# Attention over eight query blocks: own slots for the score pieces, rotating PSUM buffers, unrolled rows

## What is computed

```python
cq = jnp.einsum('bcd,bqd,d->bcq', c, q, w_cq) + b_cq
s = (c @ w_c + b_c)[:, :, None] + (q @ w_q + b_q)[:, None, :] + cq
a = jax.nn.softmax(s, axis=2)
c2q_att = jnp.einsum('bcq,bqd->bcd', a, q)
b_att = jax.nn.softmax(jnp.max(s, axis=2), axis=1)
q2c_att = jnp.einsum('bc,bcd->bd', b_att, c)[:, None, :]
x = jnp.concatenate([c, c2q_att, c * c2q_att, c * q2c_att], axis=-1)
z = x @ W_l.T + b_l
```

## Time and profile before

| | us |
|---|---|
| median of three runs | 265.16 |
| lowest, highest | 263.92, 265.46 |
| the profiled execution | 264.06 |
| its span, first to last instruction | 262.2 |
| mean granted TensorE clock | 0.895 of full |

### The profile page before, as it was taken

How to read it: one execution, slowest core, us unless ns; L and a number is a source line. 1 busy time by engine, 2 the same in 40 slices (tenths; PEclk the granted TensorE clock), 3 DMA queues, 4 the chain that set the end, 5 groups by cost and what they waited for, 6 DMA issues and landing times.

```text
span 262.2 us, 5174 instructions
## 1 busy us (share of the span) xinstructions
PE 198.8 (76%) x1721; PEld 145.0 (55%) x1721; DVE 175.6 (67%) x363; ACT 153.0 (58%) x233; POOL 136.8 (52%) x185
## 2 busy tenths in 40 slices
PE   0349699379969999999999998699841007999990
PEld 0113266236746766667666666599741006988880
DVE  2997887348979979799799796977745001545340
ACT  2289398167849788698686995892020002845430
POOL 2359999892960923907509259960001720244433
PEclk9997997869999999999999999799955555999997
DMA  6995199099998999999999989799000237000000
GB/s 230 401 347 155 40 242 266 22 226 199 248 214 207 246 221 257 242 249 253 240 256 254 257 201 257 107 228 192 0 0 0 100 125 238 4 32 17 17 23 0
DMA packets 127135, 44.68 MB, mean 170 GB/s; under 512 B 107734, under 2 KB 124910, under 8 KB 127118
## 3 DMA queue, kind: packets, MB, share of 16 engines
q1 hardware_dynamic: 126104, 42.87, 69.3%
q0 software_dynamic: 864, 1.58, 1.8%
q10 hardware_dynamic: 150, 0.00, 0.0%
HBM read 14.15 MB, written 4.01 MB: 69 GB/s over the span
## 4 chain that ended last, share of the span: by engine, by line
PE 41%; POOL 16%; issue 13%; DVE 12%; ACT 8%; DMA 7%; ACTq 0%; DVEq 0%; POOLq 0%
POOL qn L408 8%; ACT Pf L566 6%; PE psS L1116 5%; PE psO L927 5%; PE psX L927 4%; DVE S L701 3%; PE psS L912 3%; DMA PT<-Phl 3%; PE psS L914 3%; PE psS L913 3%; POOL rows_by_expert L505 3%; PE psO L930 2%; PE psS L1098 2%; PE psX L930 2%; PE psS L1101 2%
## 5 line engine op out<-in xcount | busy, mean ns | idle before, releaser
L701 DVE TENSOR_SCALAR_CACHE_REDUCE S<-psS 128x1024 f32<-128x1024 f32 (+1 forms) x56 | 61.8, 1105 | 22.5 <-ACT Pf L566 15.5
L566 ACT ACTIVATE Pf<-S,negb 128x1024 f32<-128x1024 f32 (+1 forms) x56 | 59.1, 1056 | 26.5 <-DVE negb L710 21.1
L719 DVE TENSOR_TENSOR Phl<-Pf,Phl 128x1024 f16<-128x1024 f32 x41 | 55.6, 1356 | 2.4 <-ACT Phl L582 2.4
L912 PE MATMUL psS<-qTh,gh 128*128 128x512 f16 (+1 forms) x104 | 40.3, 388 | 19.5 <-issue 6.3
L582 ACT CAST Phl<-Pf 128x1024 f16<-128x1024 f32 x48 | 50.2, 1045 | 7.7 <-DMA PT<-Phl 5.9
L445 POOL TENSOR_TENSOR Phl<-Pf,Phl 128x256 f16<-128x256 f32 x28 | 17.9, 671 | 48.0 <-ACT Phl L582 47.7
L913 PE MATMUL psS<-qTl,gh 128*128 128x512 f16 (+1 forms) x104 | 40.4, 388 | 0.0
L914 PE MATMUL psS<-qTh,gl 128*128 128x512 f16 (+1 forms) x104 | 40.4, 388 | 0.0
L927 PE MATMUL psO<-qn,PT 128*128 128x256 f16 x204 | 39.1, 284 | 0.0
L930 PE MATMUL psO<-qn,PT 128*128 128x128 f16 x204 | 37.3, 226 | 0.0
L927 PE MATMUL psX<-qn,PT 128*128 128x256 f16 x204 | 36.2, 273 | 0.0
(11 more groups left out here) (179 smaller groups left out, 373.6 us busy)
## 6 DMA issues: line engine op xcount, KB each, us to landing
stageT<-in_w SPq DMA_DIRECT2D x8, 512.0 KB, 4.3
stageT<-in_ctxT SPq DMA_DIRECT2D x6, 512.0 KB, 6.7
PT<-in_ctx SPq DMA_DIRECT2D x6, 512.0 KB, 6.8
rows_by_expert<-stageT SPq DMA_DIRECT2D x5, 385.5 KB, 3.5
S<-rows_by_expert SPq DMA_DIRECT2D x3, 514.0 KB, 6.0
PT<-Phl SPq DMA_TRANSPOSE x48, 4.0
Pf<-in_x SPq DMA_DIRECT2D x1, 512.0 KB, 4.0
stageT<-in_x SPq DMA_DIRECT2D x1, 512.0 KB, 4.4
```

The costliest lines, as they stand in the source:

```text
L566: nc.scalar.activation(Pf[:, e % 3, 0:b - a], S[:, a:b], ACT.Exp, bias=negb[:, bass.ds(t, 1)], accum_out=Lp[:, bass.ds(t * NG + e, 1)]).th ...
L701: nc.vector.tensor_scalar(out=S[:, a:b], in0=psS[n % 3][:, 0:b - a], scalar1=1.0 / GS, scalar2=None, op0=ALU.mult, op1=ALU.max, accum_out= ...
L719: nc.vector.tensor_tensor(lo, Pf[:, e % 3, 0:hi.shape[1]], hi, ALU.subtract).then_inc(low_done, 1)
L912: nc.tensor.matmul(dst, g_h, qTh[:, a:b], start=True, stop=False)
```

## The change

- `S` becomes a ring of SLOTS = 8 long slots, with two short ones (`Send`) for the short pieces. exp works in place; `Pf` is gone. An eviction waits for the low half eight long pieces back.
- `Phl` has PARTS = 4 buffers instead of three.
- PSUM buffers rotate over the whole sequence of pieces (`(u * NG + n) % 3`), so each score piece waits for the eviction three pieces back, across rows too.
- Weighted sums follow twelve pieces behind (AHEAD = 5 in the place of LAG = 4).
- DVE does `low(u-1, n-1)` ahead of `scores(u, n)`; the row's maximum comes right behind the last eviction, the short low half behind that. `attended` moves to the start of a row.
- POOL takes the low half of piece 3 only for rows 1 to 6 (0 to 6 before); in row 0 it is DVE's.
- The loops are written out on all engines.
- The fill of expert rows is issued ahead of the short transpose, not behind it. Some later buffers (`hf`, `x2T`, `xTp`, `wc2`, `ints`, `x_sb`) lie elsewhere.

```diff
@@
-    LAG = 4
+    AHEAD = 5
+    SLOTS = 8
+    PARTS = 4
+    BANKS = 3
@@
-        S = sb("S", [P, Q])
-        Pf = sb("Pf", [P, 3, GR])
-        Phl = sb("Phl", [P, 3, 2, GR], F16)
+        S = sb("S", [P, SLOTS, GR])
+        Send = sb("Send", [P, 2, QE])
+        Phl = sb("Phl", [P, PARTS, 2, GR], F16)
@@
+        def pool_low(t, e):
+            return e == 3 and 0 < t < T - 1
+        def slot(t, e):
+            return S[:, (t * (NG - 1) + e) % SLOTS, :] if e < NG - 1 else Send[:, t % 2, :]
+        def bank(u, n):
+            return psS[(u * NG + n) % BANKS]
@@ sync
-                if 1 <= t <= NB // RING:
-                    sp.wait_ge(empty_ready, 2)
...
+                    elif e == 5 and 1 <= t <= NB // RING:
+                        sp.wait_ge(empty_ready, 2)
...
@@ gpsimd
-            for e in LOW_POOL:
-                low_piece(0, e)
@@ scalar, exp_piece
-                if e >= 3:
-                    wait_low(act, t, e - 3)
-                elif not isinstance(t, int) or t > 0:
-                    wait_low(act, t - 1, (NG - 1, 4, 5)[e])
-                nc.scalar.activation(Pf[:, e % 3, 0:b - a], S[:, a:b], ACT.Exp, bias=negb[:, bass.ds(t, 1)],
+                nc.scalar.activation(slot(t, e), slot(t, e), ACT.Exp, bias=negb[:, t:t + 1],
@@ scalar, high
-                elif e >= 3:
-                    act.wait_ge(pT_landed[e - 3], 16 * (t + 1))
-                elif has_prev:
-                    act.wait_ge(pT_landed[e + 3], 16 * t)
+                elif past >= 0:
+                    act.wait_ge(pT_landed[past % (NG - 1)], 16 * (past // (NG - 1) + 1))
@@ vector, scores
-                if has_prev:
-                    dve.wait_ge(exp_done, (u - 1) * NG + n + 1)
-                    if n == 0:
-                        dve.wait_ge(negb_ready, u)
+                past = u * (NG - 1) + n - SLOTS
+                if n == NG - 1 and u >= 2:
+                    wait_low(dve, u - 2, n)
+                elif n < NG - 1 and past >= 0:
+                    wait_low(dve, past // (NG - 1), past % (NG - 1))
+                if u > 0 and n == 0:
+                    dve.wait_ge(negb_ready, u)
@@ vector, the rows
-                for e in range(NG):
-                    if e == LAG and has_prev:
-                        attended(t - 1, 1 - odd)
-                    if has_next:
-                        scores(t + 1, e, True)
-                    low(t, e)
-                if has_next:
-                    row_max(t + 1)
...
+            for u in range(1, T):
+                for n in range(NG):
+                    if n > 0:
+                        low(u - 1, n - 1)
+                    elif u > 1:
+                        low(u - 2, NG - 1)
+                    scores(u, n)
+                    if n == 0 and u > 2:
+                        attended(u - 3)
+                row_max(u)
+                if u == 1:
+                    dve.wait_ge(row_term_in_psum, 1)
+                    nc.vector.tensor_copy(row_term[:, :], psX[:, 0:T]).then_inc(row_term_ready, 1)
+            low(T - 2, NG - 1)
...
+            attended(T - 3)
@@ tensor, scores
-                    if n >= 3:
-                        pe.wait_ge(scores_out, u * NG + n - 2)
-                    elif has_prev and n == 0:
-                        pe.wait_ge(scores_out, u * NG)
-                dst = psS[n % 3][:, (c % 2) * CH:(c % 2) * CH + b - a]
+                if c % 2 == 0 and u * NG + n >= BANKS:
+                    pe.wait_ge(scores_out, u * NG + n - BANKS + 1)
+                dst = bank(u, n)[:, (c % 2) * CH:(c % 2) * CH + b - a]
@@ tensor, the rows
-            with pe.Fori(1, T - 2, 2) as t:
-                step(t, 1, True, True)
-                step(t + 1, 0, True, True)
+            for u in range(1, T):
+                if u == 2:
+                    pe.wait_ge(row_term_ready, 1)
+                    pe.wait_ge(late_gl_ready, 1)
+                for n in range(NG):
+                    if u == 1 and n == 3:
+                        row_terms()
+                    for c in range(2 * n, min(2 * n + 2, NCH)):
+                        scores(u, c)
+                    if n >= AHEAD:
+                        weighted(u - 1, n - AHEAD)
+                    elif u > 1:
+                        weighted(u - 2, NG - AHEAD + n)
@@ tensor, behind the rows
-            weighted(T - 2, 0, 3, True)
+            weighted(T - 2, 2)
+            weighted(T - 2, 3)
```

More of the change, by code:

```diff
@@ L370, in _ @@
                 for e in range(NG):
-                    transpose(t, e, t > 0)
+                    transpose(t, e)
                     if e == 2 and t < 2:
@@ L441, in low_piece @@
                 pool.wait_ge(high_done, t * NG + e + 1)
-                _, hi, lo, _ = piece(e)
+                _, hi, lo, _ = piece(t, e)
                 for a in range(0, GR, CHUNK):
                     r = slice(a, a + CHUNK)
-                    last = nc.gpsimd.tensor_tensor(lo[:, r], Pf[:, e % 3, r], hi[:, r], ALU.subtract)
+                    last = nc.gpsimd.tensor_tensor(lo[:, r], slot(t, e)[:, r], hi[:, r], ALU.subtract)
                 last.then_inc(low_pool_done, 1)
-            for e in LOW_POOL:
-                low_piece(0, e)
             pool.wait_ge(b12_landed, 64)
@@ L576, in high @@
                     act.wait_ge(consts_ready, 4)
-                elif e >= 3:
-                    act.wait_ge(pT_landed[e - 3], 16 * (t + 1))
-                elif has_prev:
-                    act.wait_ge(pT_landed[e + 3], 16 * t)
-                _, hi, _, _ = piece(e)
-                nc.scalar.copy(hi, Pf[:, e % 3, 0:hi.shape[1]]).then_inc(high_done, 1)
-            def step(t, has_prev):
+                elif past >= 0:
+                    act.wait_ge(pT_landed[past % (NG - 1)], 16 * (past // (NG - 1) + 1))
+                _, hi, _, _ = piece(t, e)
+                nc.scalar.copy(hi, slot(t, e)).then_inc(high_done, 1)
+            for t in range(T):
                 for e in range(NG):
                     exp_piece(t, e)
-                    high(t, e, has_prev)
-            step(0, False)
-            with act.Fori(1, T - 1) as t:
-                step(t, True)
-            for e in range(NG):
-                exp_piece(T - 1, e)
-                high(T - 1, e, True)
-                if e == 2:
-                    act.wait_ge(nM_ready, 1)
-                    nc.scalar.activation(eb[:, :], Mrow[:, :], ACT.Exp, bias=nM[:, :],
-                                         accum_out=es1[:, :]).then_inc(eb_ready, 1)
+                    high(t, e)
+                    if t == T - 1 and e == 2:
+                        act.wait_ge(nM_ready, 1)
+                        nc.scalar.activation(eb[:, :], Mrow[:, :], ACT.Exp, bias=nM[:, :],
+                                             accum_out=es1[:, :]).then_inc(eb_ready, 1)
             act.wait_ge(eb_ready, 1)
@@ L942, in row_terms @@
                 last.then_inc(row_term_in_psum, 1)
-            def step(t, odd, has_prev, has_next):
-                for e in range(NG):
-                    if not has_prev and e == LAG:
-                        row_terms()
-                    if has_next:
-                        for c in range(2 * e, min(2 * e + 2, NCH)):
-                            scores(t + 1, c, True)
-                    if e >= LAG:
-                        weighted(t, odd, e - LAG, has_prev)
-                    elif has_prev:
-                        weighted(t - 1, 1 - odd, NG - LAG + e, True)
             pe.wait_ge(g_ready, 2)
@@ L1054, in _ @@
             for e in (4, 5, 6):
-                weighted(T - 1, 1, e, True)
+                weighted(T - 1, e)
             turn_x2(0)
```

141 lines of the change are left out of this document (64 added, 77 removed).

## The result

The changed kernel takes 261.62 us (median of four runs, 260.9 to 262.89), beside 265.31 of the kernel before in the same session: a ratio of 0.9874, with an interval from 0.9835 to 0.9914. It is faster, by 3.7 us where 11 were forecast, and lies outside the range. The profiled execution took 260.9 us, its span is 259.1.

| stretch | before | after | moved | forecast |
|---|---|---|---|---|
| to PE's first score of row 2 | 54.17 | 49.32 | -4.9 | -5.2 |
| row 2 | 20.33 | 18.19 | -2.1 | -2.5 |
| rows 3 to 6 | 69.02 | 70.71 | +1.7 | -3.0 |
| row 7 | 16.60 | 18.56 | +2.0 | -0.1 |
| behind it | | | +0.2 | +0.1 |

A forecast was written before the change was run, and what follows sets the result against it. PE was taken as the bound, with a floor of 16.5 us a row; -5.2 - 2.5 - 3.0 - 0.1 - 0.2 + 0.3 = -10.7 us from 264.06 or 265.16 gave 254 us, range 250.5 to 258.5.

The forecast's parts named there:

- The start: Before row 2: with POOL's low half of row 0 on DVE, PE starts row 2 at 49.0 instead of 54.17, -5.2 us.
- rival C: Row 0: DVE and POOL block each other, six low halves wait 0.83 us each, giving back 5.0 us: 259 us; 8%.
- Row 2 and the borders: Row borders: all PE waits go; row 2 falls from 20.33 to 17.8 us, -2.5, later rows to 16.5.
- the 1.3 of the forecast: Row 2: PE still starts at half clock after standing idle, adding 1.3 us to the 16.5 us row.
- 15.5 us is what a row costs the queue, and 16.5 leaves 1 us: SP queue: nine issues sum to 15.5 of a 17.3 us period, so it keeps up with rows of 16.5.
- The terms of rows 3 to 6 and row 7: Late rows: without border waits, rows 3 to 6 fall from 69.02 to 66.0 us, -3.0; row 7, -0.1.
- 4 to 5 us to spare: Each row: transposes of low half 0 land 4 to 5 us before PE's weighted sums need them.
- Rival B: Rows: SP queue or DMA engines hold rows at 17.2 us, so rows 3 to 6 gain nothing: 257 to 258; 17%.
- Rival D: PE's instruction fetch: longer program, four more packets, up to 4.0 us each for a transpose held: 270, or above 265; 5%.
- cost nil: Unrolled loops: register instructions fall away, with no time charged or gained in the sum.
- The tail: Around the rows' end: one more weighted piece sticks out, +0.3; exp starts earlier through DVE's border order at row 7, -0.2.

The follow-up runs named there:

- loads_small: Changed kernel with the six weight loads among the rows cut to an eighth of their columns or less, issues kept (wrong weights): 252.42 us, ratio 0.9506.
- before_unrolled: Kernel before with PE's loop over rows 1 to 6 alone written out: 266.98 us, ratio 1.0057.
- after_near: Changed kernel with a PSUM buffer rotation that repeats every two rows instead of every three, PE still written out: 261.45 us, ratio 0.9784.
- after_looped: after_near with PE's rows 3 to 6 as a hardware loop of two rows a turn: 258.77 us, ratio 0.9773.
- loads_halved: Changed kernel with fills behind the last row and each of six weight loads issued as two halves, behind pieces 2 and 4: 254.08 us, ratio 0.9613.

## Why the prediction was wrong, point by point

*The start* was right in its mechanism and within 0.4 us: POOL's step gone, the short exp of row 0 at 45.33, the row term at 49.11, PE at 49.32. The six low halves of row 0 took 1.76, 1.22, 1.22, 1.22, 2.05 and 1.33 us; three of them:

```profile
41.73 1.22 DVE L718 TENSOR_TENSOR Phl<-S,Phl 128x1024 f16<-128x1024 f32 x1
...
44.01 2.05 DVE L718 TENSOR_TENSOR Phl<-S,Phl 128x1024 f16<-128x1024 f32 x1
...
47.13 1.33 DVE L718 TENSOR_TENSOR Phl<-S,Phl 128x1024 f16<-128x1024 f32 x1
```

so rival C's price fell: two of six lost 0.5 to 0.8 us, the others next to nothing. Its blocking was there, but mostly on the other side. POOL's subtraction beside each of the first four low halves took 1.65 to 1.69 us, against 0.66 or 0.67 for others of its size. One of them, and the one before it:

```profile
36.60 0.67 POOL L424 TENSOR_TENSOR qn<-PT,qn 128x256 f16<-128x256 f32 x1
37.24 1.68 POOL L424 TENSOR_TENSOR qn<-PT,qn 128x256 f16<-128x256 f32 x1
```

The low half of 2.05 us began at 44.01, 0.18 us behind a subtraction of POOL on `gl` that ended at 44.99. The one that starts second pays, and in row 0 that was mostly POOL, which had the time.

*Row 2 and the borders* were right as far as the queue let them: no border wait, rows of 16.5 and 16.7 at first, and in loads_small 16.5 through to the end. Row 2 gained 2.1 us of the 2.5: its granted clock was 0.50 from 50.40 to 53.81, 3.41 us, which cost 1.7 and not the 1.3 of the forecast.

*"15.5 us is what a row costs the queue, and 16.5 leaves 1 us"* is the step that failed. I took the sum of SP's issue times for the queue's work, and SP's waits for spare time. But the DMA engines still worked off what was queued while SP waited. Without the waits the same nine DMAs took 18.1 us, 17.4 of them issue time. Even by my own sum there was no spare microsecond: of the 1.8 us beside the 15.5, some 0.7 were gaps between issues, which stay when the waits go, so a row of 16.5 left 0.3 us. The period with its waits, 17.3, alone said that 16.5 was not shown to be possible; and since the stops came on top, it was no bound either.

*The terms of rows 3 to 6 and row 7* (-3.1 together) came out as +3.7. The lag that I counted as "4 to 5 us to spare" was there and was spent, 2 us a row, in rows 3 and 4. A slack delays a slower station; it does not take it from the sum.

*Rival B* named the queue, with 17 in 100, and priced it by the old row, 17.2. That row had been set by PE's border and the old buffers; the queue itself had become slower.

*Rival D* had a cause of that: four more packets on the instruction queue, "most while the DMA engines are full". It came true on a path that I didn't cost, each stopping the transposes for 1.25 to 1.7 us. I charged them 4 us each on PE and gave it 5 in 100, instead of adding four or five times a stop to the queue's sum, whether or not PE ever waited for its code. And the unrolled loops stood in the sum as "cost nil". The Trainium skill (Runtime: NRT & Kernel Launch, section Instruction fetch mechanics) says that crossing a block of 16 KB costs one bump of a DMA tail, mostly hidden, and that kernels prefer full unrolling. The 0.23 MB in 14 packets agree with its block, but none of the changed kernel's six in the rows was hidden from the transposes, and before_unrolled was 0.6% slower.

*The tail* was forecast at +0.3 and -0.2 and came out at +0.2. From the end of the rows to PE's turn of the last attended row are 27.45 us before (160.12 to 187.57) and 27.39 now (156.78 to 184.17), so the added weighted piece (1.32 us) was hidden wholly. PE waited 0.61, 0.41 and 2.15 us there before; now it waits 0.51 us, and 1.48 for a row that DVE normalises later:

```profile
159.52 0.63 PE L971 MATMUL psS<-idf,a_sb 128*128 128x128 f32 x2 [1.48 <-DVE a_sb L731]
```

What stays open: why a whole load costs the queue more than two halves, and how the 1.8 us of longer issues divide. By the single periods above the stops are 1.2 us or more of them, but no difference between the times of after_near and after_looped confirms it, and denser traffic may hold the rest.

## What to carry to other kernels

A queue's capacity is not the time its issuer is busy: take the whole period, waits included, as its cost until a stretch without waits shows less, and where a change removes waits elsewhere, ask which queue will lose its pauses. Follow the lag between producer and consumer over several rows, since slack can hide a slower queue for two of them. Written-out loops can be paid for on the DMA engines: count the instruction packets that they add, at 1.2 to 1.9 us of standing transposes each, and move fills and whole loads out of a full queue first (here 0.9613 in loads_halved, against 0.9874 of the change).
